# One kernel, eight layers: guest pieces in slots of their own, and in the state-space layer a fifth of the products on GpSimd and the convolution on TensorE

## The chip, the cores and the metric

The kernel runs on one core of one Trainium2 chip. The metric is the device time of one execution in microseconds (us), the median of three runs. Engines are named as the profile names them: PE is TensorE's matmuls and PEld its weight loads, DVE is VectorE, ACT is ScalarE, POOL is GpSimd, SP is SyncE, which here only issues transfers.

## The reference

A tensor `x` of 8 sequences of 256 tokens and 128 features goes through eight residual layers, `x = x + f(layernorm(x))`:

```
linear attention (16 heads, running sums)         -> feed-forward, 8 experts, top 2, plus a shared one
softmax attention (16 heads of 64)                -> the same feed-forward
causal attention with rotary positions (16 of 8)  -> feed-forward, 32 experts, top 4, at most 128 tokens each
state-space layer (below)                         -> the same feed-forward
```

The state-space layer, with 128 features `d` and 64 states `n`:

```
left, right = split(up_x @ W_up + b_up)
x     = silu(sum_k conv_w[:, k] * left shifted by k + conv_b)        # three taps in time
delta = softplus(x @ W_delta + b_delta)
Bm, Cm = x @ W_B + b_B, x @ W_C + b_C
h_t   = exp(delta_t * A[d, n]) * h_(t-1) + delta_t * Bm_t[n] * x_t[d]   # a scan over 256 tokens
y_t[d] = sum_n h_t[d, n] * Cm_t[n] + D_skip[d] * x_t[d]
out   = (y * silu(right)) @ W_down + b_down
```

## The kernel before

The tokens are cut into four passes of 512 (two sequences each). The eight layers run one after the other, each over its four passes; a layer's loop is its stage. In the order of the profile: linear attention (20 to 119 us), `biased_ffn` (119 to 308), `wide_attention` (308 to 666), `biased_ffn` again (666 to 857), `rotary_attention` (857 to 1081), `capped_ffn` (1081 to 1287), `state_space` (1287 to 1787) and `capped_ffn` again (1787 to 1986).

**Guests.** What has to be ready before a pass of a layer (layer norm, projections, routing) is cut into numbered pieces, `tensor(pe, p, n)`, `scalar`, `gpsimd` and `vector`, one function for each engine. While a stage works on pass p, its loop calls the pieces of its own pass p + 1, one piece number in each slot of the loop; in its last pass it calls the pieces of the next layer's first pass. `Following.slot(n)` does that, and the list `within` of the guest says how many pieces are done by each slot of its host. Every engine executes its queue in order, so a piece that has to wait holds up the host's work behind it on that engine. Between two stages all engines meet at the end of a block; SP's queue of transfers must have been issued by then.

**`capped_ffn`** has 17 slots in a pass. On PE iteration g does `up(g + 3)` (six matmuls), the guest piece, `spread_weights(g)` and `down(g - 2)`; on DVE it does `hidden(g + 3)`, `weigh(g)` and the guest piece. `route_vector` is the routing on DVE. Its part 4, in slot 11, applies the cap (four operations) and splits the weights into three bf16 parts (five operations); the PE piece of slot 13, `route_turn`, waits for the split (`r_split`) and transposes it.

**`biased_ffn`** has 9 slots. Its host loops on ACT change the table of functions for a guest's Ln and back: a layer norm's second half (`prepare_scalar(..., 1)`) waits for a PE matmul, loads a table, runs Ln and Exp, and the host loads its own table again.

**`rotary_attention`** as a guest: norm in pieces 6 to 8, four projections with their rotations in 9 to 12, in 12 also the key and its four masked copies `rot_km` on POOL, values in 13.

**`state_space`** has 64 slots, or steps, in a pass, each for two halves of the features and a fixed state group: a scan of [128, 512].

```
PE    spread_rows(i): exponent's delta -> bank DELTA[i % 3]; delta*x -> bank DELTA_X[i % 3]
ACT   exp of the first, in place
DVE   dbx(i) = bank DELTA_X * Bm (L2114); then the scan of step i - 1 (L2122)
POOL  hc(i) = h * Cm (L2078)
PE    reduce(i - 4): adds hc into bank 5 (L2024)
```

PE does `spread_rows(i)`, `reduce(i - HOLD)` and the guest piece, in this order. `spread_rows(i)` waits for the scan of i - 3, the scan of i for `hc` of i - 4. After a pass, DVE's `finish` needs all 64 reductions, and the next pass's first `reduce` waits for `gated`. The guest pieces on DVE: the convolution in three operations (17 to 19), silu in two (23, 24), the gate (25), softplus (31, 32, 36, 37), delta*x (38). `delta` and `delta*x` are split into three bf16 parts by ACT and POOL in turn (39 to 48), and then `sync` moves them into `packed` with twelve transfers on SP.

## Time and profile before

| what | value |
|---|---|
| time, median of 3 runs | 1993.4 us (1988.6 to 1994.98) |
| the profiled execution: its own time | 1988.01 us |
| its span, first to last instruction | 1986.2 us |
| PE busy | 1786.8 us, 90% |
| DVE busy | 1511.3 us, 76% |
| ACT busy | 874.8 us, 44% |
| POOL busy | 703.6 us, 35% |
| mean granted TensorE clock | 0.966 |

The busy shares are means over stages of different kinds. The granted clock has two levels, full (2.4 GHz, shown as 1.00) and half (1.2 GHz, shown as 0.50); a value between is a stretch with both. In a line of the timeline the number in brackets is how long the engine had been idle before, and what released it. A wait for several semaphores is put down to one of them.

### The profile page before, as it was taken

The numbers are of one execution on the slowest core, as the hardware profiler recorded it, in microseconds if no ns is written. First come the engines' busy times: TensorE is split into PE (matmuls) and PEld (weight loads), VectorE is DVE, ScalarE is ACT, GpSimd is POOL, SyncE is SP. The second block draws the span as 40 slices with busy tenths as digits, with TensorE's granted clock in tenths as the row PEclk, the third lists the DMA queues.
The fourth block names the chain that finished last, engine by engine and source line by source line (L and its number), as shares of the span: only waits on it lengthen the run. The fifth ranks groups of instructions, "written<-read, shape, count | busy, mean of one in ns | idle before, by whom it ended". The sixth has DMA issues, their size and how long they took to land. (4 is left out here: it accounts for less than half of the span.)

```text
span 1986.2 us, 23692 instructions
## 1 busy us (share of the span) xinstructions
PE 1786.8 (90%) x7574; PEld 932.4 (47%) x7581; DVE 1511.3 (76%) x2501; ACT 874.8 (44%) x2063; POOL 703.6 (35%) x802
## 2 busy tenths in 40 slices
PE   7879999999998999989998999888888888789999
PEld 2346654555554555546665555432222323225555
DVE  5868865555555588657767888699999999997887
ACT  3345544654545454345653333444354443333332
POOL 4722222333333222322220000077678686660000
PEclk9989999999999999979998999899999999999999
DMA  6000000000000000010000000000000000000000
GB/s 244 1 1 0 1 0 1 1 1 1 1 1 1 0 1 1 0 43 2 1 2 1 1 0 1 17 0 13 5 0 17 0 15 2 0 0 1 0 6 16
DMA packets 9787, 19.94 MB, mean 10 GB/s; under 512 B 1088, under 2 KB 8384, under 8 KB 8768
## 3 DMA queue, kind: packets, MB, share of 16 engines
q1 hardware_dynamic: 9664, 18.42, 2.7%
q8 instruction: 62, 1.02, 0.2%
q14 instruction: 61, 0.50, 0.1%
HBM read 14.22 MB, written 1.05 MB: 8 GB/s over the span
## 5 line engine op out<-in xcount | busy, mean ns | idle before, releaser
L2078 POOL TENSOR_TENSOR ssm_hc<-ssm_h,ssm_cm 128x512 f32<-128x512 f32 x256 | 334.6, 1309 | 155.2 <-DVE ssm_h L2122 154.9
L2122 DVE TENSOR_TENSOR_SCAN ssm_h<-banks,ssm_dbx 128x512 f32<-128x512 f32 x256 | 310.6, 1214 | 2.3 <-DVE ssm_dbx L2114 2.3
L307 PE MATMUL banks<-ffn_x_high,up_high 128*128 128x512 f32 x544 | 283.5, 521 | 13.9 <-ACT ffn_s1g L856 9.6
L2024 PE MATMUL banks<-ssm_hc,const 128*128 128x512 f32 x512 | 272.9, 615 | 12.2 <-DVE ssm_gated L2099 9.3
L2062 ACT ACTIVATE banks<-banks,a_neg 128x510 f32<-128x510 f32 x256 | 167.1, 659 | 248.0 <-PE banks L2011 247.1
L308 PE MATMUL banks<-ffn_x_low,up_high 128*128 128x512 f32 x544 | 216.9, 399 | 0.0
L309 PE MATMUL banks<-ffn_x_high,up_low 128*128 128x512 f32 x544 | 216.5, 398 | 0.0
L1498 POOL TENSOR_SCALAR wide_pin<-wide_pin,wide_rden 128x256 f32<-128x256 f32 x256 | 117.6, 478 | 226.1 <-DVE wide_rden L1516 226.1
L2114 DVE TENSOR_TENSOR ssm_dbx<-banks,ssm_bm 128x512 f32<-128x512 f32 x256 | 171.9, 672 | 13.5 <-PE banks L2014 11.4
L343 POOL TENSOR_TENSOR x_norm<-x_centred,x_square 128x512 f32<-128x512 f32 x32 | 41.3, 1291 | 395.1 <-ACT x_square L338 395.1
L1731 ACT ACTIVATE ffn_th<-banks 128x512 f32<-128x512 f32 (+1 forms) x136 | 81.1, 597 | 212.4 <-PE banks L309 190.2
L2011 PE MATMUL banks<-ssm_packed,half 96*128 96x510 bf16 x256 | 103.0, 402 | 75.8 <-DVE ssm_h L2122 71.1
L307 PEld LDWEIGHTS banks<-ffn_x_high,up_high 128*128 128x128 f32 x544 | 103.3, 190 | 103.1 <-issue 43.7
L1156 ACT ACTIVATE rot_pin<-banks,rot_low 128x128 f32<-128x128 f32 (+1 forms) x256 | 104.1, 419 | 99.9 <-DVE rot_low L1238 99.9
L2011 PEld LDWEIGHTS banks<-ssm_packed,half 96*128 96x128 bf16 x256 | 25.1, 98 | 256.8 <-DVE ssm_h L2122 231.2
L1696 PE MATMUL banks<-ffn_a,weights 128*128 128x512 f32 (+1 forms) x272 | 141.2, 602 | 0.0
L1767 DVE SCALAR_TENSOR_TENSOR ffn_p<-ffn_th,banks 128x512 f32<-128x512 f32 (+1 forms) x136 | 92.8, 683 | 59.2 <-ACT ffn_th L1731 58.4
L308 PEld LDWEIGHTS banks<-ffn_x_low,up_high 128*128 128x128 f32 x544 | 103.7, 191 | 50.9 <-issue 35.8
L2024 PEld LDWEIGHTS banks<-ssm_hc,const 128*128 128x128 f32 x512 | 100.0, 198 | 57.9 <-POOL ssm_hc L2078 20.3
L1472 ACT ACTIVATE wide_pin<-banks,wide_low 128x256 f32<-128x256 f32 x256 | 117.5, 478 | 13.4 <-DVE wide_low L1530 13.4
L882 POOL TENSOR_SCALAR ffn_hg<-ffn_hg 128x512 f32<-128x512 f32 x72 | 45.1, 627 | 203.4 <-DVE ffn_hg L904 202.1
L309 PEld LDWEIGHTS banks<-ffn_x_high,up_low 128*128 128x128 f32 x544 | 103.4, 190 | 25.4
(230 smaller groups left out, 3373.6 us busy)
## 6 DMA issues: line engine op xcount, KB each, us to landing
ssm_packed<-ssm_parts SPq DMA_DIRECT2D x48, 64.0 KB, 2.0
up_whole<-in_up SPq DMA_DIRECT2D x1, 2304.0 KB, 15.1
weights<-in_weights SPq DMA_DIRECT2D x1, 2048.0 KB, 22.4
up_whole<-in_up SPq DMA_DIRECT2D x1, 2048.0 KB, 8.5
half<-in_half SPq DMA_DIRECT2D x1, 1440.0 KB, 17.8
weights<-in_weights SPq DMA_DIRECT2D x1, 1168.0 KB, 24.7
weights<-in_weights SPq DMA_DIRECT2D x1, 1152.0 KB, 8.1
const<-in_const SPq DMA_DIRECT2D x1, 1042.0 KB, 10.0
```

The lines of the kernel that those rows point to most:

```text
L307: pe.matmul(out, w_high, x_high, start=True, stop=False)
L308: pe.matmul(out, w_high, x_low, start=False, stop=False)
L309: return pe.matmul(out, w_low, x_high, start=False, stop=True)
L1472: ins = act.activation(pin[:, i % RING, m, cols], k.bank[2 * (i % 2) + m][:, cols], ACT.Exp, bias=low[:, i % RING, n:n + 1], accum_out=den ...
L1498: ins = pool.tensor_scalar(part, part, rden[:, i % RING, n:n + 1], 1.0, ALU.mult, ALU.mult)
L1696: pe.matmul(k.bank[5][:], w("sd" if n == 0 else f"d{n - 1}")[0:rows, :], a[0:rows, g % (LAG + 1), :], start=(n == 0), stop=(n == N - 1)).t ...
L2011: pe.matmul(two(k.bank[DELTA[i % AHEAD]])[:, :, 1:], pick, two(packed[0:96, p % 2, 0, g, :])[:, :, 1:], start=True, stop=True) \
L2024: pe.matmul(k.bank[5][:], k.c("hot")[:, P - row:2 * P - row], hc[:, i % HOLD, :], start=(i % NP == 0), stop=(i % NP == NP - 1)).then_inc(s ...
L2062: act.activation(spot_i, spot_i, ACT.Exp, scale=k.a_neg[:, i % NP:i % NP + 1]).then_inc(s["da"], 1)
L2078: pool.tensor_tensor(hc[:, i % HOLD, :], h[:, i % HOLD, :], cm[:, i // NP % 2, :], ALU.mult) \
L2114: dve.tensor_tensor(dbx[:, i % AHEAD, :], k.bank[DELTA_X[i % AHEAD]][:], bm[:, i // NP % 2, :], ALU.mult) \
L2122: dve.tensor_tensor_scan(h[:, n % HOLD, :], k.bank[DELTA[n % AHEAD]][:], dbx[:, n % AHEAD, :], 0.0, ALU.mult, ALU.add).then_inc(s["h"], 1)
```

## The change

**Routing.** `route_vector` has seven parts instead of six: the split is a part of its own. In `capped_ffn` it moves from slot 11 to slot 12; `route_turn` stays in slot 13. In `biased_ffn` it stays in the same slot. The `within` lists of the guests are moved to fit, above all `biased_ffn` in `wide_attention`, whose pieces 3, 4, 5, 6 go to slots 10, 11, 12, 13 (before 8, 11, 13, 14 with 5 and 6 both in 14).

**Rotary guest.** ACT's half of the norm runs one slot behind PE's, all pieces behind it one later, and `rot_km` is made in two pairs in two more slots.

**State space.** Twelve of 64 products in a pass (steps 4, 9, ... 59) leave DVE: ACT copies the bank to `dxs`, POOL multiplies by Bm into `pdbx`, after `hc` of four steps earlier. PE's two spreads are issued apart, the one of delta*x a step earlier. The convolution is three fp32 matmuls with diagonal weights; ACT moves the result out with bias and the factor 0.5, so silu is one operation on DVE; `u = 1 + e` goes to ACT. The table for tanh is loaded in piece 19, the one for Ln in piece 34. The second and third split parts move from 43 to 48 to 47 to 54, and `sync` issues four transfers behind each part instead of twelve behind the last. `a_neg` is computed while the layer is a guest.

```
@@ route_vector
             link(dve.tensor_tensor(cw, cw, buf["rank"][:], ALU.mult))
+    if n == 5:
         link(dve.tensor_copy(part(0), buf["cw"][:]))
...
-    if n == 5:
+    if n == 6:
         dve.wait_ge(s["r_turned"], p + 1)
@@ biased_ffn, capped_ffn
-        for part in {4: (0,), 5: (1,), 6: (2, 3, 4), 7: (5,)}.get(n, ()):
+        for part in {4: (0,), 5: (1,), 6: (2, 3, 4, 5), 7: (6,)}.get(n, ()):
...
-"wide": (0,) * 7 + (1, 3, 3, 3, 4, 4, 5, 7, 8)},
+"wide": (0,) * 7 + (1, 3, 3, 4, 5, 6, 7, 7, 8)},
...
-        if n in (5, 6, 7, 8, 11, 13):
+        if n in (5, 6, 7, 8, 11, 12, 13):
@@ rotary_attention
-        if n == 7:
+        if n == 8:
             prepare_scalar(k, act, s, p, 1)
...
-            for c in range(4):
+        for c in {14: (0, 1), 15: (2, 3)}.get(n, ()):
...
-{"ffn0": (7, 8, 9, 10, 11, 12, 13, 14, 16)}
+{"ffn0": (7, 8, 10, 11, 12, 13, 14, 15, 16)}
@@ wide_attention
+                if follow.done >= 5:
+                    pe.wait_ge(nxt.s["r_diff"], 1)
@@ state_space, sync
-        sp.wait_ge(s["split"], 6 * (p + 1))
-        for g in range(4):
-            for part in range(3):
+        for part in range(3):
+            sp.wait_ge(s["split"], 6 * p + 2 * part + 2)
+            for g in range(4):
@@ state_space, guest pieces
+        if n == 19:
+            pe.wait_ge(s["right_in"], p + 1)
+            pe.wait_ge(s["cleared"], 1)
+            for tap in range(3):
+                ins = pe.matmul(two(k.bank[7]), w(f"conv{tap}"), left[:, :, tap:L + tap],
+                                start=(tap == 0), stop=(tap == 2))
+            ins.then_inc(s["conv"], 1)
...
+        if n == 20:
+            act.wait_ge(s["conv"], p + 1)
+            act.activation(conv[:], k.bank[7][:], ACT.Identity, bias=half_b[:], scale=0.5).then_inc(s["conv_in"], 1)
+        if n == 19:
+            k.table(act, "exp_and_others")
...
-            link(dve.scalar_tensor_tensor(conv[:], tc[:], 1.0, conv[:], ALU.add, ALU.mult))
-        if n == 24:
-            dve.tensor_scalar(xs[:, p % 2, :], conv[:], 0.5, None, ALU.mult).then_inc(s["x"], 1)
+            dve.scalar_tensor_tensor(xs[:, p % 2, :], tc[:], 1.0, conv[:], ALU.add, ALU.mult).then_inc(s["x"], 1)
@@ state_space, loop: PE, ACT, POOL, DVE
             for i in range(ALL + HOLD):
+                if i + 1 < ALL:
+                    spread_dx(i + 1)
                 if i < ALL:
-                    spread_rows(i)
+                    spread_delta(i)
...
+                if i + 1 < ALL and by_pool(i + 1):
+                    m = pooled[i + 1]
+                    act.wait_ge(s["bx"], i + 2)
...
+                    act.activation(dxs[:, m % 2, :], k.bank[DELTA_X[(i + 1) % AHEAD]][:], ACT.Copy).then_inc(s["dx_in"], 1)
...
+                j = i + AHEAD + 1
+                if j < ALL and by_pool(j):
+                    m = pooled[j]
+                    pool.wait_ge(s["dx_in"], m + 1)
...
+                    pool.tensor_tensor(pdbx[:, m % 2, :], dxs[:, m % 2, :], bm[:, j // NP % 2, :], ALU.mult) \
+                        .then_inc(s["pdbx"], 1)
...
-                if i < ALL:
-                    dve.wait_ge(s["bc"], 2 * i + 2)
+                if i < ALL and not by_pool(i):
+                    dve.wait_ge(s["bx"], i + 1)
```

## Rows read from the trace of the kernel before

**Rows 1.** Windows: us, busy time (instructions) by engine, clock, DMA; state-space stage.

```profile
1287.00:1787.00 500.00, 410.10 (x1102) 147.15 (x1102) 479.89 (x591) 211.42 (x329) 352.26 (x272) 0.96 0.02 6
```

**Rows 2.** Timeline of DVE: start, length, line; state-space stage, convolution and silu.

```profile
1319.57 1.21 DVE L2122 TENSOR_TENSOR_SCAN ssm_h<-banks,ssm_dbx 128x512 f32<-128x512 f32 x1
...
1321.86 1.22 DVE L2122 TENSOR_TENSOR_SCAN ssm_h<-banks,ssm_dbx 128x512 f32<-128x512 f32 x1
...
1326.73 1.22 DVE L2122 TENSOR_TENSOR_SCAN ssm_h<-banks,ssm_dbx 128x512 f32<-128x512 f32 x1
...
1328.44 1.22 DVE L2122 TENSOR_TENSOR_SCAN ssm_h<-banks,ssm_dbx 128x512 f32<-128x512 f32 x1
...
1332.16 1.21 DVE L2122 TENSOR_TENSOR_SCAN ssm_h<-banks,ssm_dbx 128x512 f32<-128x512 f32 x1
...
1334.60 1.21 DVE L2122 TENSOR_TENSOR_SCAN ssm_h<-banks,ssm_dbx 128x512 f32<-128x512 f32 x1
...
1336.64 1.21 DVE L2122 TENSOR_TENSOR_SCAN ssm_h<-banks,ssm_dbx 128x512 f32<-128x512 f32 x1
```

**Rows 3.** Chain that ended last, by time: start, length; second capped_ffn.

```profile
1834.35 0.42 PE banks L387 x4
...
1840.53 0.86 PE banks L1696 x2
...
1850.87 0.87 PE banks L322 x2
```

**Rows 4.** Timeline of POOL, state-space stage, end of its guest work in a pass.

```profile
1360.88 1.63 POOL L2078 TENSOR_TENSOR ssm_hc<-ssm_h,ssm_cm 128x512 f32<-128x512 f32 x1 [0.80 <-DVE ssm_h L2122]
...
1373.20 1.26 POOL L2078 TENSOR_TENSOR ssm_hc<-ssm_h,ssm_cm 128x512 f32<-128x512 f32 x1
1374.42 1.16 POOL L1941 TENSOR_TENSOR ssm_rest<-ssm_dx,ssm_parts 128x512 f32<-128x512 f32 x1
```

**Rows 5.** Waits of the state-space stage: total us, times, longest.

```profile
ACT ssm_parts L1931 <- POOL ssm_rest L1941: 23.5, 12, 3.1
```

**Rows 6.** Instructions with the tile ssm_gated: ns min/median/max.

```profile
L2099 DVE SCALAR_TENSOR_TENSOR ssm_gated<-ssm_y,ssm_gate x4: 692/1218/1220, 1415.2 to 1788.0; 128x512 f32<-128x512 f32 x4
```

**Rows 7.** Timeline between two passes of the state-space stage.

```profile
1415.21 1.22 DVE L2099 SCALAR_TENSOR_TENSOR ssm_gated<-ssm_y,ssm_gate 128x512 f32<-128x512 f32 x1
...
1416.58 1.75 PE L2024 MATMUL banks<-ssm_hc,const 128*128 128x512 f32 x2 [3.09 <-DVE ssm_gated L2099]
...
1420.70 0.69 DVE L2114 TENSOR_TENSOR ssm_dbx<-banks,ssm_bm 128x512 f32<-128x512 f32 x1 [2.54 <-PE banks L2014]
```

**Rows 8.** Timeline of SP, then ACT and PE, at the start of that stage.

```profile
1279.22 7.78 SPq L1848 DMA_DIRECT2D ssm_packed<-ssm_parts  x12
...
1287.74 0.26 ACT L2056 ACTIVATE a_neg<-weights 128x64 f32<-128x64 f32 x1 [7.24 <-PEq L1610]
...
1288.36 0.61 PE L2011 MATMUL banks<-ssm_packed,half 96*128 96x510 bf16 x1 [4.58 <-DVE banks L2093]
```

**Rows 9.** Timeline of capped_ffn, slots 11 to 13 of a pass.

```profile
1832.89 0.23 DVE L449 CAST r_split<-r_cw 128x128 bf16<-128x128 f32 x1
...
1834.21 0.68 DVE L1767 SCALAR_TENSOR_TENSOR ffn_p<-ffn_th,banks 128x512 f32<-128x512 f32 x1
...
1834.35 0.42 PE L387 MATMUL banks<-half,r_split 128*96 128x128 bf16 x4 [0.94 <-DVE r_split L453]
...
1836.12 0.68 DVE L1767 SCALAR_TENSOR_TENSOR ffn_p<-ffn_th,banks 128x512 f32<-128x512 f32 x1
```

**Rows 10.** Windows: stretches with and behind a wait of PE.

```profile
1256.50:1259.90 3.40, 3.40 (x6) 1.63 (x5) 1.81 (x3) 0.69 (x1) 0.00 (x0) 0.50 0.00 0
1832.00:1838.00 6.00, 5.06 (x20) 2.23 (x19) 5.66 (x15) 1.19 (x2) 0.00 (x0) 1.00 0.00 0
...
813.50:819.50 6.00, 6.00 (x14) 3.95 (x14) 4.57 (x7) 2.90 (x5) 1.84 (x3) 0.50 0.01 3
```

**Rows 11.** Timeline of PE in the first capped_ffn, last pass.

```profile
1255.80 1.46 PE L1873 MATMUL banks<-ssm_xs,weights 128*128 128x512 f32 x2 [2.34 <-DVE ssm_xs L1964]
```

**Rows 12.** Timeline of the second biased_ffn, guest norm and last pass's end.

```profile
813.47 0.79 PE L307 MATMUL banks<-ffn_x_high,up_high 128*128 128x512 f32 x1 [3.35 <-ACT ffn_s1g L856]
...
843.81 2.69 POOL L1016 TENSOR_SCALAR rot_km<-rot_k,const 128x512 f32<-128x512 f32 x4
...
850.38 3.84 PE L823 MATMUL banks<-ffn_a,weights 128*128 128x512 f32 x4 [5.12 <-DVE ffn_a L923]
```

**Rows 13.** Timeline of PE in wide_attention, last pass.

```profile
639.86 1.97 PE L1412 MATMUL banks<-wide_pt,wide_va 128*64 128x256 f32 x8 [4.75 <-DVE wide_pt L1525]
```

More of the change, by code:

```diff
@@ L1821, in state_space @@
     ALL = PASSES * NP
-    s = k.semaphores("ssm", ["left", "left_in", "right", "right_in", "tanh_r", "conv", "tanh_c", "x", "delta", "z", "e", "u",
+    by_pool = lambda i: i % NP % 5 == 4
+    pooled = [0]
+    for i in range(ALL):
+        pooled.append(pooled[-1] + by_pool(i))
+    steps = [i for i in range(ALL) if by_pool(i)]
+    s = k.semaphores("ssm", ["bx", "dx_in", "pdbx", "halved", "cleared", "conv_in", "left", "left_in", "right", "right_in", "tanh_r", "conv", "tanh_c", "x", "delta", "z", "e", "u",
                              "ln", "b", "b_in", "c", "c_in", "gate", "ready", "rest", "split", "packed0", "packed1", "packed2", "packed3",
@@ L1885, in scalar @@
             act.wait_ge(k.w_loaded[G], 16)
+            act.activation(k.a_neg[:], w("a_log"), ACT.Exp).then_inc(s["a"], 1)
         if n == 7:
@@ L1911, in scalar @@
             act.activation(e[:], e[:], ACT.Exp, scale=-1.0).then_inc(s["e"], 1)
+        if n == 30:
+            act.wait_ge(s["e"], p + 1)
+            act.activation(u[:], e[:], ACT.Identity, bias=1.0).then_inc(s["u"], 1)
         if n == 31:
@@ L1915, in scalar @@
         if n == 34:
+            k.table(act, "natural_log_exp_and_others")
             act.wait_ge(s["c"], p + 1)
@@ L1986, in run, with programs @@
         dbx = sb("ssm_dbx", [P, AHEAD, T])
+        dxs, pdbx = sb("ssm_dxs", [P, 2, T]), sb("ssm_pdbx", [P, 2, T])
         h, hc = sb("ssm_h", [P, HOLD, T]), sb("ssm_hc", [P, HOLD, T])
         with nc.Block(no_gpsimd_drain=True) as block:
[L1989 to L1991 removed]
+            programs(nxt, block, y, gated, dbx, dxs, pdbx, h, hc)
+    def programs(nxt, block, y, gated, dbx, dxs, pdbx, h, hc):
         @block.sync
@@ L2009, in spread_rows, with spread_dx @@
                     pe.wait_ge(s["h"], i - AHEAD + 1)
-                pick = k.h("pick")[0:96, c * P:(c + 1) * P]
-                pe.matmul(two(k.bank[DELTA[i % AHEAD]])[:, :, 1:], pick, two(packed[0:96, p % 2, 0, g, :])[:, :, 1:],
-                          start=True, stop=True) \
-                    .then_inc(s["bc"], 1)
-                pe.matmul(k.bank[DELTA_X[i % AHEAD]][:], pick, packed[0:96, p % 2, 1, g, :], start=True, stop=True) \
-                    .then_inc(s["bc"], 1)
+                pe.matmul(two(k.bank[DELTA[i % AHEAD]])[:, :, 1:], k.h("pick")[0:96, c * P:(c + 1) * P],
+                          two(packed[0:96, p % 2, 0, g, :])[:, :, 1:], start=True, stop=True).then_inc(s["bc"], 1)
+            def spread_dx(i):
+                (g, c), p = spot(i), i // NP
+                if c == 0:
+                    pe.wait_ge(s[f"packed{g}"], 16 * 3 * (p + 1))
+                if i >= AHEAD and by_pool(i - AHEAD):
+                    pe.wait_ge(s["dx_in"], pooled[i - AHEAD + 1])
+                elif i >= AHEAD:
+                    pe.wait_ge(s["dbx"], i - AHEAD + 1 - pooled[i - AHEAD + 1])
+                pe.matmul(k.bank[DELTA_X[i % AHEAD]][:], k.h("pick")[0:96, c * P:(c + 1) * P],
+                          packed[0:96, p % 2, 1, g, :], start=True, stop=True).then_inc(s["bx"], 1)
             def reduce(i):
@@ L2296 @@
     lay(5, "b_right", m["b_up"][P:, None])
-    lay(5, "conv_w", m["conv_w"])
+    for tap in range(3):
+        lay(5, f"conv{tap}", np.diag(m["conv_w"][:, tap]))
     lay(5, "conv_b", m["conv_b"][:, None])
```

103 lines of the change are left out of this document (51 added, 52 removed).

## The prediction, made before the changed kernel ran

> **What bounds the kernel now.** I read the busy time by stage first, then the timeline inside the stages that the change touches. The state-space stage is the longest, 500 us, and DVE is busy for 479.9 of them, PE for 410, POOL for 352 and ACT for 211 [rows 1]. In its timeline the scans follow each other: between two bare steps 1.71 us from start to start, of which the scan takes 1.13 and the product 0.58, and each guest operation of DVE pushes the next scan back by its own length [rows 2]. So time taken from DVE here is time taken from the kernel, until POOL or PE is next. The `capped_ffn` stages are different. The chain of waits runs there through PE from `route_turn` (L387) over `down` (L1696) to the next norm (L322), 16.5 us in which a matmul follows a matmul [rows 3]. What delays `route_turn` delays the kernel.
>
> **The products.** 48 of 256 leave DVE: 48 x 0.58 = 27.8 us less. What can take it back is POOL. Two of its operations in a row are 1.22 us apart for `hc`, 1.1 for the split's [rows 4]. A pass with guests then costs POOL 64 + 12 + 1 operations at 1.22 and 4 at 1.1, 98 us. DVE's pass is 64 x 1.13 + 52 x 0.58 = 102.5 and about 6 for its guests and `finish`. POOL has 0.7 us of slack in five steps (8.0 against 6 x 1.22 = 7.3). Steps 43 to 50 hold two pairs of split operations and two products: followed, the product of step 54 lands 0.7 us after its scan could start. I take 0.8 us in each of three passes, +2.5, bounds 0 and +20 (a rival below). ACT's 48 copies lie in its idle time.
>
> The Trainium skill (GPSIMD Engine Reference, Performance versus the Vector engine) keeps elementwise work on VectorE, GpSimd being 1.96 times slower. The rows here say 1.22 against 0.58, 2.1 times. By that rule the move is a bad trade, 58.6 us of POOL for 27.8 of DVE; by the rows of the stage POOL has 148 us idle and DVE 20, and I go with these.
>
> **DVE's guests.** Three taps of the convolution stretch three steps to 7.16 us where bare ones take 5.14: 2.02. Silu's two operations stretch two steps to 4.48 against 3.43, and the second alone costs 0.33 [rows 2]; the new silu keeps the first. `u` is of the second's kind, 0.33. That is 2.02 + 0.33 + 0.33 = 2.7 us in a pass, 8.0 in the three passes hosted here. The three matmuls are 3 x 0.87 = 2.6 us of PE in one slot [rows 3]; PE runs more than 2 us ahead of the scan, so I cost them at nothing here.
>
> **The shared path of DVE and POOL.** `gated`, which reads two SBUF tensors, takes 0.69 us once and 1.22 in three of four cases, with POOL at work [rows 6], and `hc` takes 1.63 instead of 1.26 beside such a guest of DVE [rows 4]. Today these guests start as a scan ends, when POOL is mostly idle; with POOL at 90% they will meet it halfway. Seven such operations in three passes, every second one late by 0.53: +5.6 us, bounds 0 and 11. The Trainium skill (SBUF — State Buffer, on the shared port pair) says that the pair is locked for a whole instruction and the loser blocks; the two lengths agree with it, and by it a meeting could cost up to a whole POOL operation.
>
> **Smaller waits of the stage.** ACT waits 23.5 us for POOL's split operations in 12 waits of up to 3.1 us [rows 5], some of which hold back the exponentials and through them a scan (0.4 us twice in a pass). Four to six slots between writer and reader remove these: -2. Between two passes the first `reduce` waits 3.09 us for `gated`, and DVE's product then 2.54 us for the spread queued behind it [rows 7]. With delta*x spread a step earlier, and step 68 a pooled one, DVE gets a step further before it stops: -1.1 at each of three borders, -3.3.
>
> **Start of the stage.** SP issues its twelve transfers in 7.78 us, until 1287.0, and the block can't end before; ACT starts at 1287.74 and PE, after `a_neg` and the resets, at 1288.36. PE had been idle since 1283.8 [rows 8]. With eight transfers issued behind the earlier parts, four remain, 2.6 us, done by 1281.8; the block ends with PE and DVE near 1283.9. -3.4 us.
>
> **The split behind part 4 of the routing.** Today DVE begins the split at 1832.89, goes on with `hidden(15)` at 1834.21, and PE, idle for 0.94 us, starts `route_turn` at 1834.35. The next `hidden` begins at 1836.12, so one `hidden` and one `weigh` take 1.91 us [rows 9]. The split now stands behind these two in DVE's queue, and PE still asks for it in slot 13, where its `up(16)` is already done. PE's wait grows from 0.94 to 2.85 us. All behind it is PE's own chain [rows 3], so the 1.91 us are paid: three passes in each of two stages, 6 x 1.91 = +11.5. Bursts on DVE get smaller, but DVE isn't what the 16.5 us behind wait for.
>
> Such a wait has a second price. PE waits 2.34 us at 1253.5 [rows 11], and the stretch 1256.5 to 1259.9 is granted 0.50 of the clock; after the 3.35 us at 810 it is 813.5 to 819.5; around today's 0.94 us the clock stays at 1.00 [rows 10]. A 2.85 us wait is between the two longer ones. With 3.4 us at half speed PE does 1.7 us less: 6 x 1.7 = +10.2, bounds 0 and +20.
>
> **Rotary guest in the second `biased_ffn`.** PE waits 3.35 us for `s1`, because ACT sits in the norm's second half (its wait, two table loads, Ln, Exp) [rows 12]. A slot later the matmul is long done, ACT's 3.9 us fall where PE works on `up(31)`, and wait and half clock go: 3.35 + 3.4 = -6.7, bounds -3 and -7. At the stage's end PE waits 5.12 us; the clamp that it needs stood behind `rot_km`, 2.69 us on POOL [rows 12]. Two at a time, behind two clamps: -2.5, bounds -1 and -4.
>
> **Routing guest in `wide_attention`.** Slot 14 holds all of the routing, 4.2 us of DVE without a pause, and PE waits 4.75 us [rows 13], then runs at half clock. In slots 12 and 13 I expect 1.6 and 0.9 us instead: 2.2 less, and some of the clock back. -4, bounds -2 and -7.
>
> **State-space guest in the first `capped_ffn`.** The convolution adds 2.6 us to PE where PE is the bound. Against that, one round of two table loads goes, which was behind the 2.34 us [rows 11]: of it I leave 0.9, and with it goes the half clock, 1.7. Loading Ln's table before a wait saves about 0.5. Sum -1.0, bounds -4 and +2.6.
>
> **The sum.** -27.8 + 2.5 - 8.0 + 5.6 - 2.0 - 3.3 - 3.4 + 11.5 + 10.2 - 6.7 - 2.5 - 4.0 - 1.0 = -28.9 us, on the profiled execution's 1988.0: 1959.1. The median of the runs is 5.4 us above that execution. From the median it would be 1964.5; I predict 1963, between the two and nearer the median.
>
> **Rivals.**
>
> *The turn costs little.* The clock may hold through a wait of 2.85 us (the windows at 0.50 begin behind the wait, and two cases are few), and DVE's other meetings with POOL may be free. Then -28.9 - 10.2 - 5.6 = -45: 1948. For it: no spell after 0.94 us. Against: two of two longer waits have one. 0.2.
>
> *POOL becomes the bound of the state-space stage.* POOL waits in order for a copy that comes over PE and ACT, and PE waits for POOL's `hc` in the `reduce` ahead of that spread. Once POOL lags, this circle (reduce 0.87, a guest matmul 0.87, spread 0.2, copy 0.66, hand-overs 0.3: 2.9 us) is longer than the 2.44 us of two POOL operations that cover it. If that gives back half of the 27.8 us and a little more, the result is -12: 1980. For it: slack of only 0.7 us in five steps. Against: without guests the lag never builds up. 0.2.
>
> *Slower.* The same circle, if it never recovers: a POOL wait of w in every period of five steps makes the period 7.3 + w, and with w above 1.3 us it is as long as today's 8.57. All 27.8 us are then gone, and from w = 1.4 on the kernel is slower; at w = 2, 51 x 0.7 = 36 us are added and the result is about 2029. The circle above gives w of at most 0.5 from rows. 0.06, other causes included.
>
> *The change does nothing that can be measured*, as where the losses in `capped_ffn` (up to 32 us) meet a half-lost gain: within 6 us (0.3%, about what this kernel's measurement can tell) of 1993. 0.05.
>
> **How the numbers follow.** The forecast (1951 to 1974) has 0.49, the two milder rivals 0.2 and 0.2. Both are faster by over 0.3%: 0.89. The range 1944 to 1982 leaves out about 2 in 10: the slower case, no change, and the outer parts of the two rivals.
>
> **What the profile after would show.** Right: bare scans 1.13 us apart twelve times in a pass; the state-space stage near 467 us with DVE above 90% and POOL near 85%; PE idle between the stages under 1.5 us; at L387 in `capped_ffn` a wait of 2.8 us six times, with 0.50 of the clock soon after, and each such stage 10 us longer; no wait of 3.35 us before `up(31)` in the second `biased_ffn`. Wrong: DVE waiting for POOL's product or for `da` at most pooled steps (then POOL is the bound), a turn that waits 1 us, or guests of DVE that keep their lengths.

## The result, and the profile after

| kernel | median | ratio to before, 95% interval | profiled span |
|---|---|---|---|
| before, timed beside it | 1989.5 us (1988.5 to 1995.0, 5 runs) | | 1986.2 us |
| changed | 1978.7 us (1976.2 to 1981.6, 5 runs) | 0.9944 (0.9927 to 0.9961) | 1976.9 us |

The change makes the kernel 0.56% faster, 10.9 us, where 30 us were predicted. First the page of the changed kernel, its line of busy time:

```profile
PE 1798.7 (91%) x7598; PEld 946.4 (48%) x7605; DVE 1485.6 (75%) x2434; ACT 901.3 (46%) x2117; POOL 755.8 (38%) x850
```

Where the time went, stage by stage. Each stage ends with the first of two matmuls that follow its last residual; their start times, before and after, cut the two traces at the same places:

| stage | before | after | difference | forecast |
|---|---|---|---|---|
| linear attention and first `biased_ffn` | 307.4 | 309.7 | +2.3 | 0 |
| `wide_attention` | 354.3 | 349.1 | -5.2 | -4.0 |
| second `biased_ffn` | 193.7 | 187.9 | -5.8 | -9.2 |
| `rotary_attention` | 224.1 | 225.0 | +0.9 | 0 |
| first `capped_ffn` | 203.7 | 210.6 | +6.9 | +9.8 |
| `state_space` | 507.7 | 487.6 | -20.1 | -36.4 |
| second `capped_ffn` | 190.9 | 202.6 | +11.7 | +10.8 |

Most of what is missing, 16 us of 20, is missing in the state-space stage. The windows of the changed kernel (columns as in [rows 1]), first that stage, then stretches of PE at half clock:

```profile
1282.50:1770.10 487.60, 416.14 (x1126) 160.28 (x1125) 456.80 (x531) 239.48 (x382) 402.88 (x320) 0.95 0.02 6
...
1166.50:1173.30 6.80, 6.47 (x12) 2.03 (x13) 3.18 (x7) 0.59 (x1) 0.00 (x0) 0.51 0.00 0
1221.20:1224.60 3.40, 3.40 (x6) 0.75 (x4) 1.07 (x3) 0.56 (x1) 0.00 (x0) 0.54 0.00 0
1815.10:1818.50 3.40, 3.40 (x9) 1.29 (x8) 1.95 (x4) 0.00 (x0) 0.00 (x0) 0.54 0.00 0
1866.30:1873.10 6.80, 6.43 (x12) 2.02 (x13) 3.23 (x7) 0.59 (x1) 0.00 (x0) 0.52 0.01 2
1920.90:1924.30 3.40, 3.40 (x6) 0.85 (x5) 1.60 (x3) 0.00 (x0) 0.00 (x0) 0.53 0.00 0
838.90:862.80 23.90, 20.27 (x84) 10.20 (x83) 9.26 (x16) 8.78 (x34) 6.63 (x7) 0.51 0.25 89
```

DVE is busy 94% of the state-space stage and POOL 83%, much as forecast; the stage is 487.6 us all the same. So the loss isn't to be seen in busy shares.

**The turn.** The timeline of DVE, then of PE, where [rows 9] had 0.94 us:

```profile
1813.39 0.22 DVE L450 CAST r_split<-r_cw 128x128 bf16<-128x128 f32 x1
...
1814.56 0.23 DVE L454 CAST r_split<-r_rest 128x128 bf16<-128x128 f32 x1
```

```profile
1814.84 0.66 PE L387 MATMUL banks<-half,r_split 128*96 128x128 bf16 x4 [2.85 <-DVE r_split L454]
```

The wait is there six times, 2.83 to 2.85 us, and behind five of the six stands one of the half-clock windows above (the first, at 1113.8, has none). The forecast for the wait was 2.85 us.

**The state-space stage**, timeline of SP, PE and DVE at its start:

```profile
1281.53 1.24 SPq L1859 DMA_DIRECT2D ssm_packed<-ssm_parts  x2
...
1283.75 0.61 PE L2039 MATMUL banks<-ssm_packed,half 96*128 96x512 bf16 x2 [0.87 <-DVE banks L2132]
...
1285.45 1.22 DVE L2165 TENSOR_TENSOR_SCAN ssm_h<-banks,ssm_dbx 128x512 f32<-128x512 f32 x1
```

The first scan starts 3.2 us behind the end of the stage before; in the kernel before it was 7.7: -4.5 (forecast -3.4); SP is no longer behind the others, as it was in [rows 8]. At the borders between two passes, timelines of PE and DVE:

```profile
1406.49 2.05 PE L2049 MATMUL banks<-ssm_hc,const 128*128 128x512 f32 x2 [3.55 <-DVE ssm_gated L2138]
```

```profile
1404.88 1.46 DVE L2138 SCALAR_TENSOR_TENSOR ssm_gated<-ssm_y,ssm_gate 128x512 f32<-128x512 f32 x1
...
1410.71 0.69 DVE L2153 TENSOR_TENSOR ssm_dbx<-banks,ssm_bm 128x512 f32<-128x512 f32 x1 [1.52 <-PE banks L2039]
```

PE's wait is longer than the 3.09 us of [rows 7], in part by the longer `gated` (1.46 us instead of 1.22); DVE's is 1.52 instead of 2.54, as the spread a step earlier was to bring. The loss comes behind all this. One place in the first pass shows how, in the timelines of POOL, PE and DVE, steps 14 to 21:

```profile
1309.53 1.27 POOL L343 TENSOR_TENSOR x_norm<-x_centred,x_square 128x512 f32<-128x512 f32 x1
1310.75 3.72 POOL L2110 TENSOR_TENSOR ssm_hc<-ssm_h,ssm_cm 128x512 f32<-128x512 f32 x3
1316.35 1.27 POOL L2123 TENSOR_TENSOR ssm_pdbx<-ssm_dxs,ssm_bm 128x512 f32<-128x512 f32 x1 [1.88 <-ACT ssm_dxs L2091]
```

```profile
1310.85 1.12 PE L1877 MATMUL banks<-x_norm,weights 128*128 128x512 f32 x2 [1.32 <-POOL x_norm L343]
...
1317.85 2.74 PE L1885 MATMUL banks<-ssm_left,weights 128*128 128x512 f32 x6
```

```profile
1312.23 0.69 DVE L2153 TENSOR_TENSOR ssm_dbx<-banks,ssm_bm 128x512 f32<-128x512 f32 x1 [1.11 <-PE banks L2039]
...
1316.91 1.22 DVE L2165 TENSOR_TENSOR_SCAN ssm_h<-banks,ssm_dbx 128x512 f32<-128x512 f32 x1 [0.79 <-issue]
...
1320.84 0.69 DVE L2153 TENSOR_TENSOR ssm_dbx<-banks,ssm_bm 128x512 f32<-128x512 f32 x1 [0.99 <-PE banks L2039]
```

A late POOL gives `x_norm` late, PE waits for it with the spreads queued behind, and DVE waits for the spread; a few steps on the six instructions of the convolution, 2.74 us on PE, do the same. And DVE's guests with two SBUF inputs are longer (groups: ns min/median/max; first `fix` in the kernel before, then the changed kernel):

```profile
L1974 DVE SCALAR_TENSOR_TENSOR ssm_fix<-ssm_u,ssm_e x4: 669/672/684, 1266.3 to 1597.7; 128x512 f32<-128x512 f32 x4
```

```profile
L1986 DVE SCALAR_TENSOR_TENSOR ssm_gate<-ssm_gate,ssm_right x4: 684/1352/1356, 1258.7 to 1570.2; 128x512 f32<-128x512 f32 x4
...
L1990 DVE SCALAR_TENSOR_TENSOR ssm_fix<-ssm_u,ssm_e x4: 684/1568/1583, 1267.7 to 1582.9; 128x512 f32<-128x512 f32 x4
...
L1995 DVE SCALAR_TENSOR_TENSOR ssm_delta<-ssm_z,ssm_fix x4: 691/1126/1128, 1272.9 to 1593.2; 128x512 f32<-128x512 f32 x4
...
L2138 DVE SCALAR_TENSOR_TENSOR ssm_gated<-ssm_y,ssm_gate x4: 691/1461/1466, 1404.9 to 1767.9; 128x512 f32<-128x512 f32 x4
```

The 684 ns are from `capped_ffn`, where POOL is idle. `ssm_gated` was 1218 in [rows 6]; `gate`, `fix` and `delta` took 0.67 us in this stage of the kernel before; they take 1.35, 1.57 and 1.13 now. A timeline of POOL and DVE shows one such meeting:

```profile
1342.43 1.27 POOL L2123 TENSOR_TENSOR ssm_pdbx<-ssm_dxs,ssm_bm 128x512 f32<-128x512 f32 x1
1342.67 1.58 DVE L1990 SCALAR_TENSOR_TENSOR ssm_fix<-ssm_u,ssm_e 128x512 f32<-128x512 f32 x1
```

`fix` begins inside POOL's operation, which ends at 1343.70, and ends 0.55 us behind it. All 15 guests of the first three passes that begin inside an operation of POOL do so, five in a pass; in the kernel before it was the three `gated` alone.

**A measure for the stage.** From the start of the first scan to that of the last there are 255 intervals. Bare, they would take 255 x 1.71 = 436.05 us, less 0.58 for each pooled product. What a kernel needs beyond that I call its excess. Two pairs of runs below have the same code in this stage (69.6 and 71.3, 40.7 and 38.6), so differences of 2 us in it say nothing. It comes from this group of DVE, before and after (read the two times behind the durations):

```profile
L2122 DVE TENSOR_TENSOR_SCAN ssm_h<-banks,ssm_dbx x256: 1194/1214/1225, 1290.9 to 1783.4; 128x512 f32<-128x512 f32 x128
```

```profile
L2165 DVE TENSOR_TENSOR_SCAN ssm_h<-banks,ssm_dbx x208: 1191/1212/1225, 1285.4 to 1763.3; 128x512 f32<-128x512 f32 x104
```

492.5 - 436.05 = 56.4 us before, 477.9 - (436.05 - 27.8) = 69.6 us after. The measure takes the forecast's 27.8 us for the bare pattern as given; in the trace 30 of the 48 intervals without a product on DVE are near 1.13 us, and the other 18 are in the excess. The excess grew by 13.2, where the forecast's terms (guests -8.0, split -2.0, borders -3.3, POOL late +2.5, meetings +5.6) had it shrink by 5.2.

### The profile page after: what moved, and what is told of

The parts are those of the page before. It is cut to its first block and busy times, and to the rows that moved or that the text cites. A ratio compares the mean times of both kernels' runs of the same rounds, so it can differ in the third digit from the quotient of the medians.

```text
span 1976.9 us, 23849 instructions
## 1 busy us (share of the span) xinstructions
PE 1798.7 (91%) x7598; PEld 946.4 (48%) x7605; DVE 1485.6 (75%) x2434; ACT 901.3 (46%) x2117; POOL 755.8 (38%) x850
## 5 line engine op out<-in xcount | busy, mean ns | idle before, releaser
L2110 POOL TENSOR_TENSOR ssm_hc<-ssm_h,ssm_cm 128x512 f32<-128x512 f32 x256 | 327.3, 1296 | 58.0 <-DVE ssm_h L2165 57.0
L2049 PE MATMUL banks<-ssm_hc,const 128*128 128x512 f32 x512 | 281.2, 631 | 33.9 <-POOL ssm_hc L2110 23.1
L307 PE MATMUL banks<-ffn_x_high,up_high 128*128 128x512 f32 x544 | 282.6, 519 | 10.3 <-ACT ffn_s1g L857 6.2
L2165 DVE TENSOR_TENSOR_SCAN ssm_h<-banks,ssm_dbx 128x512 f32<-128x512 f32 x208 | 249.4, 1211 | 10.6 <-ACT banks L2094 5.5
L2153 DVE TENSOR_TENSOR ssm_dbx<-banks,ssm_bm 128x512 f32<-128x512 f32 x208 | 138.9, 668 | 11.6 <-PE banks L2039 10.8
L2049 PEld LDWEIGHTS banks<-ssm_hc,const 128*128 128x128 f32 x512 | 98.6, 200 | 79.0 <-POOL ssm_hc L2110 56.4
L2039 PE MATMUL banks<-ssm_packed,half 96*128 96x512 bf16 x256 | 100.8, 394 | 7.8 <-DVE ssm_dbx L2153 6.5
```

What stands on the lines that cost most here:

```text
L307: pe.matmul(out, w_high, x_high, start=True, stop=False)
L2049: pe.matmul(k.bank[5][:], k.c("hot")[:, P - row:2 * P - row], hc[:, i % HOLD, :], start=(i % NP == 0), stop=(i % NP == NP - 1)).then_inc(s ...
L2110: pool.tensor_tensor(hc[:, i % HOLD, :], h[:, i % HOLD, :], cm[:, i // NP % 2, :], ALU.mult) \
L2153: dve.tensor_tensor(dbx[:, i % AHEAD, :], k.bank[DELTA_X[i % AHEAD]][:], bm[:, i // NP % 2, :], ALU.mult) \
L2165: dve.tensor_tensor_scan(h[:, n % HOLD, :], k.bank[DELTA[n % AHEAD]][:], product, 0.0, ALU.mult, ALU.add).then_inc(s["h"], 1)
```

## The experiments

Each run has the kernel before timed beside it; the ratios are what is compared. The scans and the excess come from one profiled execution, which is within 2.5 us of the median except with the convolution on DVE (8.5 us under it) and the early spread (3.8 under).

| run | median us | ratio, 95% | scans, us | excess |
|---|---|---|---|---|
| changed kernel | 1978.7 | 0.9944 (0.9927 to 0.9961) | 477.9 | 69.6 |
| split in slot 11 | 1960.1 | 0.9854 (0.9842 to 0.9867) | 479.6 | 71.3 |
| no pooled products | 1977.6 | 0.9938 (0.9926 to 0.9951) | 476.8 | 40.7 |
| convolution on DVE | 1979.7 | 0.9949 (0.9933 to 0.9966) | 476.0 | 67.8 |
| convolution in three slots | 1978.4 | 0.9947 (0.9935 to 0.9959) | 479.3 | 71.1 |
| exponential first | 1985.0 | 0.9984 (0.9975 to 0.9993) | 483.4 | 75.2 |
| early spread | 1978.2 | 0.9952 (0.9936 to 0.9969) | 474.1 | 65.9 |
| idle operations on POOL | 1990.3 | 1.0003 (0.9991 to 1.0016) | 489.4 | 53.4 |
| quiet places, split in 11 | 1944.5 | 0.9781 (0.9766 to 0.9795) | 462.6 | 47.9 |
| quiet places in all passes | 1940.1 | 0.9756 (0.9738 to 0.9775) | 460.2 | 43.8 |
| busy places | 1961.0 | 0.9862 (0.9844 to 0.9880) | 481.2 | 66.6 |
| quiet, convolution on DVE | 1941.0 | 0.9766 (0.9747 to 0.9785) | 462.5 | 44.4 |
| split in 11, no products | 1954.0 | 0.9828 (0.9809 to 0.9847) | 474.6 | 38.6 |

**The split in slot 11.**

```
-        if n in (5, 6, 7, 8, 11, 12, 13):
+        for part in {5: (0,), 6: (1,), 7: (2,), 8: (3,), 11: (4, 5), 13: (6,)}.get(n, ()):
```

> The changed kernel with one thing undone: in capped_ffn the split (part 5 of the routing on DVE) stands in slot 11 again, behind part 4, and no longer in slot 12 behind hidden and weigh. Theory 'the turn waits behind one hidden and one weigh, and pays for it twice': PE's wait ahead of route_turn falls from 2.85 us to about 0.94 in all six passes, 6 x 1.91 = 11.5 us less, and the stretches of half clock behind it (five of the six have one, 3.4 or 6.8 us long, 23.9 us together) go as well, 12 us less. Together 23 us less than the changed kernel: near 1956 us, ratio to the kernel before 0.983. Rival 'only the wait counts': the half-clock stretches have other causes and stay, 11.5 us less, near 1967, ratio 0.9886. Rival 'the turn isn't on the path': less than 3 us.

The ratio falls by 0.0090, 18 us. The first `capped_ffn` goes from 210.6 to 200.2 us and the second from 202.6 to 191.2: 21.8 us, of which 6 x 1.91 = 11.5 are the wait; the remaining 10.3 go with the half-clock windows, which are gone. The state-space stage gave 2.5 back. The waits of the second `capped_ffn` for the split (total us, times, longest), changed kernel and this one:

```profile
PE banks L387 <- DVE r_split L454: 8.5, 3, 2.9
```

```profile
PE banks L387 <- DVE r_split L454: 2.8, 3, 0.9
```

Inside either `capped_ffn` no stretch is at half clock now, but for the first 2 us of the second. Both prices of the turn hold.

**No pooled products.**

```
-    by_pool = lambda i: i % NP % 5 == 4
+    by_pool = lambda i: False
```

> The changed kernel without the twelve pooled products in a pass: all 256 products on DVE, no copies to dxs, everything else as changed. By the terms of the forecast (48 products 27.8 us, of which the shared path took 5.6 and a late POOL 2.5 back) it is 19.7 us slower than the changed kernel: 1998 us, ratio 1.004. By the reading of the changed kernel's trace, in which the guests of DVE are longer by some 9 us in sum, the steps of the norm by 2 and the steps of the split by 4.3, it is only about 12 us slower: 1990 us, ratio 1.000. If POOL is truly the bound of the stage the products are worth nothing and it is within 3 us of the changed kernel. In the trace the lengths of the fix, gate and delta operations on DVE should fall from 1.57, 1.35 and 1.13 us back to 0.67 if POOL's products are what they meet; the burst of six convolution matmuls should still push the scans back (by 2.3 us in a pass), if PE's short lead is the cause.

The time is that of the changed kernel. 27.8 us more of work on DVE, 28.9 us less excess. Of the cases in the expectation it is the last: the products are worth nothing. The groups of the guests:

```profile
L1986 DVE SCALAR_TENSOR_TENSOR ssm_gate<-ssm_gate,ssm_right x4: 662/663/683, 1260.9 to 1569.3; 128x512 f32<-128x512 f32 x4
...
L1990 DVE SCALAR_TENSOR_TENSOR ssm_fix<-ssm_u,ssm_e x4: 661/662/684, 1269.8 to 1581.8; 128x512 f32<-128x512 f32 x4
```

They are back at 0.66 us, so POOL's products are what made them long. The convolution costs 1.09 us a pass, not the 2.3 that I expected: half of its loss was POOL's too. The excess by place, us, worked out from the starts of the 256 scans (guest pieces of the first three passes; the last pass apart):

| steps, with their guests | before | changed | no products | quiet, all passes |
|---|---|---|---|---|
| 0 to 6, border | 17.1 | 13.3 | 11.9 | 10.0 |
| 7 to 13, norm | 0.0 | 2.5 | 0.3 | 0.0 |
| 14, 15, projection behind x_norm | 2.7 | 4.7 | 0.0 | 0.2 |
| 16 to 20, convolution | 6.1 | 7.1 | 3.3 | 6.4 |
| 21 to 25, silu, gate | 5.3 | 6.2 | 3.6 | 3.6 |
| 26 to 38, softplus | 9.1 | 12.0 | 8.0 | 8.0 |
| 39 to 63, split | 3.2 | 7.9 | 0.2 | 1.6 |
| last pass, from step 7 | 12.8 | 15.9 | 13.3 | 13.9 |

The third column against the first is the change without its headline: 15.7 us less excess. The second against the third is what 48 products cost: something at every guest.

**The convolution, back on DVE, or in three slots of PE.**

```
-        if n == 19:
+        if n in (19, 20, 21):
...
-            for tap in range(3):
...
+            pe.matmul(two(k.bank[7]), w(f"conv{tap}"), left[:, :, tap:L + tap],
+                      start=(tap == 0), stop=(tap == 2)).then_inc(s["conv"], 1)
...
```

These are the three slots of PE. The version on DVE has the three taps in its pieces 17 to 19 again.

> The changed kernel with the convolution on DVE again, three taps in pieces 17 to 19 (with halved weights, so that silu stays one operation), and no conv matmuls and no copy on ACT. Theory 'PE has no lead to spare': the three matmuls hold up the spreads behind them, and the scans around them lose 0.87 + 1.46 = 2.33 us in each of the three passes; taps on DVE cost 2.04. So the state-space stage changes by less than 1.5 us in sum, and the first capped_ffn, where PE is the bound, is 2.6 us shorter: 2 to 4 us less than the changed kernel, 1975 us. The forecast's pricing (matmuls free, taps 2.02 each pass) says 6.1 - 2.6 = 3.5 us more: 1982 us.

> The changed kernel with the three convolution matmuls in three slots (pieces 19, 20, 21) instead of all in 19, and ACT's copy, its tanh and silu one or two pieces later. Theory 'PE has no lead to spare': a slot then needs 1.30 + 0.87 = 2.17 us of PE against 1.71 of DVE, so PE falls back by 0.46 in each of three slots instead of 2.2 at once; the scans of these steps lose about 0.9 us in a pass instead of 2.33: 3 to 4 us less than the changed kernel in three passes, 1975 us. The forecast's view (the matmuls were free anyway) says no difference, within 1 us. A rival within the theory: as DVE runs at PE's pace there, it could save nothing, if each of the three slots takes 2.17 us.

On DVE: no difference in time that can be told (0.9949 against 0.9944). The trace has the 2.9 us less in the first `capped_ffn` (207.7), but the taps don't cost 2.04 us a pass. The group:

```profile
L1976 DVE SCALAR_TENSOR_TENSOR ssm_conv<-ssm_left,ssm_half_w,ssm_conv x4: 753/1534/1539, 1246.9 to 1553.0; 128x512 f32<-128x512 f32 x4
```

1.53 us instead of 0.73, since with a product on POOL in every fifth step the taps meet it too; they cost 3.84 us a pass, 4.4 us more in three passes than the matmuls. The steps of the split lose 3.0 us instead of 7.9 in that trace, so the sum hardly moves; why was not looked into. In three slots: no gain; the steps behind lost what the burst had lost (excess 71.1). That was the rival within the theory. Neither place is better while POOL is late.

**The order of copy and exponential, and the circle.**

```
+                act.wait_ge(s["bc"], i + 1)
...
+                act.activation(spot_i, spot_i, ACT.Exp, ...).then_inc(s["da"], 1)
                 if i + 1 < ALL and by_pool(i + 1):
...
```

> The changed kernel with ACT's exponential of step i ahead of the copy to dxs for step i + 1, instead of behind it. A copy holds an exponential back by 0.5 to 0.6 us. Theory 'the exponentials behind a copy are late' (interval 17 of each pass, 0.87 us, and interval 7, up to 1.09): most of 2.6 + 2.0 us comes back, 3 us less than the changed kernel. Theory 'POOL's time is what runs out': the copy comes 0.6 us later to a POOL that is late anyway, so what the exponentials gain POOL loses: within 1.5 us of the changed kernel.

```
-                if i + 1 < ALL:
+                if i + 1 < ALL and not by_pool(i + 1):
                     spread_dx(i + 1)
                 if i < ALL:
                     spread_delta(i)
+                if i + 2 < ALL and by_pool(i + 2):
+                    spread_dx(i + 2)
...
```

> The changed kernel with PE's spread of delta*x for a pooled step issued one slot earlier, ahead of a reduce and a guest matmul instead of behind them, and ACT's copy right behind the exponential two steps ahead. This cuts the circle hc, reduce, guest, spread, copy, product. Theory 'the circle is what costs': POOL's 26.2 us of waiting for dxs fall below 8, PE waits less for hc, and the state-space stage is 8 to 12 us shorter (1968 us). Theory 'POOL's occupied time is what costs' (a product makes POOL late for the next steps, and whatever guest falls there pays): the waits for dxs go, but the scans hardly move, 0 to 3 us less.

How long POOL's product waited for the copy (us, times), in the changed kernel, with the exponential first, and with the early spread:

```profile
POOL ssm_pdbx L2123 <- ACT ssm_dxs L2091: 26.0, 17, 3.2
```

```profile
POOL ssm_pdbx L2123 <- ACT ssm_dxs L2094: 55.0, 39, 3.7
```

```profile
  ACT ssm_dxs L2096: 9.4, 13
```

A copy 0.6 us later is worse by 5.6 us of excess, and outside both cases that I gave (0.9984, and 6 us more in the median): POOL's lateness matters more than an exponential's. The early spread takes two thirds of the waits away and shortens the scans by 3.8 us in its trace, in the medians nothing (0.9952 against 0.9944). So the circle over reduce, guest, spread and copy is at most some 4 of the 29 us. What of the rest is POOL's occupied time alone?

**Idle operations on POOL.**

```
-    by_pool = lambda i: i % NP % 5 == 4
+    by_pool = lambda i: False
...
+                if i % NP % 5 == 0 and i % NP < 60:
+                    pool.tensor_tensor(pdbx[:, i // 5 % 2, :], bm[:, i // NP % 2, :], cm[:, i // NP % 2, :], ALU.mult)
```

> The kernel without pooled products (all 256 on DVE), but with twelve operations of the same size a pass on POOL (Bm * Cm into pdbx, which nobody reads), at the places where the products stood. They wait for nothing and nobody waits for them, so this measures what POOL's time alone costs, without the copy on ACT and the way over PE. In the kernel without products the stage's scans had 40.7 us above the bare pattern, with products 69.6. Theory 'POOL's occupied time costs': most of the 28.9 us is here too, 15 to 25 us more than without products, 1993 to 2003 us. Theory 'the circle over PE and ACT costs': only the meetings of DVE's two-input guests with POOL are paid, 7 us, and something for x_norm behind an operation: 6 to 10 us, 1984 to 1988 us. Since DVE has more work here (no product less), POOL has 0.6 us more in five steps, which speaks for the lower end of either.

1990.3 us: 12.7 more than without them, 12.7 in the excess as well (53.4 against 40.7). That lies between the two expectations. 3.9 of it is in the softplus steps, where `fix` and `delta` meet POOL again, 3.1 in the split's, 2.9 in the last pass. So 48 operations that nobody waits for cost DVE 0.26 us each. The other 16.2 us of the products' 28.9 come with their being needed: scans wait for them, ACT has a copy each, and DVE, 0.58 us faster in five steps, leaves POOL less time to catch up. Which of the three has how much wasn't taken apart.

**Places for the products.** If a product costs by what falls behind it, it is a matter of where it stands. POOL runs the product of step j behind `hc(j - 4)` and is late for some steps from there. Free of guests are only eight places in a pass:

```
...
-    by_pool = lambda i: i % NP % 5 == 4
+    QUIET = ((4, 9, 20, 30, 43, 49, 55, 59, 63), (12, 20, 30, 43, 49, 55, 59, 63), (12, 20, 30, 43, 49, 55, 59, 63),
+             (4, 9, 14, 19, 24, 29, 34, 39, 44, 49, 54, 59))
+    by_pool = lambda i: i % NP in QUIET[i // NP]
```

> The split of capped_ffn in slot 11, and pooled products only where no guest falls into the four steps before: steps 12, 20, 30, 43, 49, 55, 59, 63 of the second and third pass, these with 4 and 9 for 12 and 20 of the first, every fifth as before in the last (where the guests are capped_ffn's). 37 products instead of 48. Theory 'a product costs by what falls into the steps behind it': 37 x 0.58 = 21.5 us are taken from DVE and about a third goes back, so 12 to 16 us less than with every fifth (1960): 1944 to 1948 us, ratio 0.978. If the products cost what they give wherever they stand, it is 1960 again, and if the last pass or the borders are where the losses lie, 1955.

1944.5 us, 0.9781: as expected. Then the last pass in the same manner (9, 14, 19, 37, 41, 49, 54, 59, 63), and against it the control with products just ahead of guests:

> The version with quiet places (1944.5 us) with two changes: in the first pass step 12 instead of 9, and in the last pass steps 9, 14, 19, 37, 41, 49, 54, 59, 63, away from the border and from capped_ffn's pieces on DVE (34 products in all). Theory 'a product costs by what falls into the steps behind it': the first pass loses 0.5 us of its excess, the last 4 of its 21.5 us, against 3 x 0.58 = 1.7 us of products given up: 2.5 to 3 us less, 1942 us, ratio 0.9765. If the places in the last pass are without influence, 1.7 us more: 1946 us.

> The version with quiet places again with the same number of products (37), but in the first three passes at places where a guest falls right behind each: steps 8, 15, 21, 27, 34, 39, 47, 53 (and 4 in the first pass) instead of 12, 20, 30, 43, 49, 55, 59, 63. Theory 'a product costs by what falls into the steps behind it': its 8 products a pass give back about what they take, as with every fifth (0.6 to 0.7 us each), so it is 25 x 0.6 = 12 to 16 us slower than the quiet version: 1957 to 1960 us, ratio 0.985. Theory 'only the number counts' (48 are too many for POOL, 37 are not): the same as the quiet version within 2 us, 1944 us.

> The quiet version with the better last pass and with the convolution on DVE again, and no product at step 20, whose wake would fall on the taps (31 products). The taps should now be as short as in the kernel before, 2.04 us in a pass instead of the 1.7 to 1.8 that the burst of six matmuls costs in the quiet version; in the first capped_ffn PE has 2.6 us less: 3 x 0.3 + 3 x 0.58 - 2.6 = 0, so the same as the quiet version with the better last pass, within 1.5 us. If the taps meet POOL anyhow (3.84 us a pass, as with every fifth product), 5 us slower than it.

> The changed kernel with the split of capped_ffn in slot 11 and no pooled products at all. It is the base against which the quiet version (34 products, ratio 0.9756) and the version with busy places (37 products, ratio 0.9862) are to be read. If the two edits are independent, it is 18 us less than without products (ratio 0.9938 - 0.0090 = 0.985, 1959 us). Then the 34 products at quiet places are worth 19 of their 19.7 us, and 37 at busy places nothing. If it comes out near 0.976 instead, the quiet version owes its gain to something else.

The groups of scans in the version quiet in all passes, and in the one with busy places (from the first start of the one line to the last of the two):

```profile
L2167 DVE TENSOR_TENSOR_SCAN ssm_h<-banks,ssm_dbx x222: 1193/1209/1225, 1276.4 to 1735.5; 128x512 f32<-128x512 f32 x111
L2167 DVE TENSOR_TENSOR_SCAN ssm_h<-banks,ssm_pdbx x34: 1194/1209/1225, 1282.7 to 1736.6; 128x512 f32<-128x512 f32 x34
```

```profile
L2167 DVE TENSOR_TENSOR_SCAN ssm_h<-banks,ssm_dbx x219: 1189/1208/1225, 1276.8 to 1758.0; 128x512 f32<-128x512 f32 x110
```

460.2 and 481.2 us. The medians are 1940.1 us (1942 expected) and 1961.0 (1957 to 1960). Against the same kernel without products (38.6 of excess, 0.9828), 34 quiet products give 19.7 us and cost 5.3: 14.4 net, and the ratios say 0.0072, 14.3 us. 37 at busy places give 21.5 and cost 28.1: a loss of 6.6, and the ratios say 0.0034, 6.8 us. The nearest pair has 37 products each and the same last pass: quiet places 1944.5 us with 47.9 of excess, busy places 1961.0 with 66.6. It is the place, not the number. My base was 5 us too high, and with it the worth that I expected of the quiet ones (19 us).

The traces do say how the excess divides into longer operations of DVE and idle time of DVE. Windows from the first scan to the last (columns as in [rows 1]), in this order: changed kernel, no products, idle operations; and, with the split in slot 11, no products, quiet in all passes, busy places:

```profile
1285.45:1763.27 477.82, 409.52 (x1109) 158.50 (x1109) 452.10 (x522) 238.71 (x381) 400.40 (x318) 0.95 0.02 6
1287.62:1764.38 476.76, 406.43 (x1109) 150.48 (x1109) 469.21 (x570) 215.56 (x333) 345.84 (x270) 0.97 0.02 6
1287.57:1777.04 489.47, 412.78 (x1109) 154.82 (x1109) 478.58 (x570) 215.78 (x333) 402.11 (x318) 0.95 0.02 5
...
1278.00:1752.61 474.61, 406.20 (x1109) 151.15 (x1109) 468.07 (x570) 215.55 (x333) 345.77 (x270) 0.97 0.02 6
1276.40:1736.57 460.17, 398.02 (x1108) 154.09 (x1107) 448.91 (x536) 231.40 (x367) 382.70 (x304) 0.97 0.02 6
1276.80:1758.02 481.22, 407.23 (x1109) 157.39 (x1109) 460.74 (x533) 234.90 (x370) 388.33 (x307) 0.95 0.02 5
```

| against the same kernel without products | DVE busy longer | DVE idle longer |
|---|---|---|
| products in every fifth step | 452.1 + 27.8 - 469.2 = 10.7 | 25.7 - 7.6 = 18.2 |
| idle operations | 9.4 | 3.3 |
| 34 quiet products | 448.9 + 19.7 - 468.1 = 0.6 | 11.3 - 6.5 = 4.7 |
| 37 products, busy places | 460.7 + 21.5 - 468.1 = 14.1 | 20.5 - 6.5 = 13.9 |

So POOL's time alone costs mostly by meetings, and what needed products add to it is nearly all waiting of DVE.

The convolution on DVE makes no difference here (0.9766). The taps are as short as before, since POOL is idle beside them:

```profile
L1978 DVE SCALAR_TENSOR_TENSOR ssm_conv<-ssm_left,ssm_half_w,ssm_conv x4: 725/727/750, 1237.2 to 1535.0; 128x512 f32<-128x512 f32 x4
```

The version that is quiet in all passes, 1940.1 us, beats both kernels: 2.4% under before, 1.9% under the changed one.

## Why the prediction was off

**Right.** The start of the stage (-4.5, forecast -3.4), the borders (17.1 to 13.3 us, -3.8, forecast -3.3), the turn (11.5 of wait and about 10 of clock, forecast 11.5 and 10.2), and, in the kernel without products, the split's steps (-3.0, forecast -2.0) and the small guests of DVE (silu and softplus -2.8, forecast -2.0). The routing guest in `wide_attention` has the right sign, and PE's wait is 2.04 us there instead of the 4.75 of [rows 13]; its size isn't settled. The stage is 5.2 us shorter here (forecast -4), but the 13 traces with this code have 349.1 to 353.4 us, in the median 352.2, 2.1 us under the one trace of the kernel before.

**The step that failed** is the paragraph "The products" with "The shared path". It gave back 2.5 us for a late POOL and 5.6 for meetings, 8.1 together. Measured, by leaving the products out: 28.9, all that they bring. Of these 10.7 are longer operations of DVE, against the 5.6 for meetings, and 18.2 are idle time of DVE, against the 2.5 for a late POOL. I weighed POOL against DVE by sums, over a pass and over five steps, found 0.7 us of slack, and followed only steps 43 to 50. What I found there came out in two of the three passes, where the scan of step 54 waits 0.71 and 0.74 us for its product. The other places were left out. POOL follows DVE step by step, and after an extra 1.22 us it is late for two or three steps, as it gains 1.71 - 1.22 = 0.49 us in each. Whatever stands in these steps pays: a guest on DVE that meets it (0.2 to 0.9 us longer), a projection behind `x_norm`, a burst on PE, the split. With products in every fifth step and guests in every second or third, nearly each product has such a neighbour.

Within that, the meetings were counted as every second of seven in a pass at 0.53 us. The trace has five of the seven in every pass, longer than before by 0.2 (`xs`, `gated`) to 0.9 us (`fix`), 7.4 us in three passes; the other two keep their length. The last pass brings 1.5 us more; what is left of the 10.7 is small and spread out. The Trainium skill (SBUF — State Buffer, on the shared port pair) says that a DVE operation with two SBUF inputs and a GpSimd one that reads SBUF exclude each other for a whole instruction; the trace agrees, 0.67 us where `fix` begins ahead of POOL's operation against 1.57 where it begins inside one, and 0.55 us from the end of the one to the end of the other. By the rule of the Trainium skill that elementwise work belongs on VectorE (GPSIMD Engine Reference, Performance versus the Vector engine) the products were a bad trade. As the change places them, they are an even one; at quiet places, a good one.

**The second step that failed**: "PE runs more than 2 us ahead of the scan, so I cost them at nothing here". A spread waits for the scan or the product of three steps ago, so PE can't be further ahead than that, and its own 1.30 us in a step of 1.71 (two spreads of 0.22 and a reduce of 0.87 from start to start) leave it 0.41 us a step to catch up. The burst costs 1.09 us a pass even with an idle POOL (3.3 us in three), more with products. That this short lead is the cause fits the burst, the three slots and the version on DVE, none of which gains; no run gave PE a longer lead. With the taps' 6.1 us gone the convolution gives 2.8 us with an idle POOL, not 6.1; as it was changed, it gives nothing (7.1 us against 6.1).

**The rival** "POOL becomes the bound" named the total (1980) and the stage, and said for it the circle. The circle is at most some 4 us, so that its total came out is luck. What it left out is that POOL's time alone costs DVE 12.7 us, and that waits come behind guests too. The sign that the prediction gave for this rival, DVE waiting at most pooled steps, did not show either: scans wait 26 times in the changed kernel, 12 of them at one of the 48 pooled steps or the step ahead of one, and twice for a product.

**Terms off in size.** The second `biased_ffn` gained 5.8 us instead of 9.2. The 3.35 us wait is gone, but at the end of the stage PE still waits twice, and the half clock behind it stays (838.9 to 862.8 above). Timelines of PE and of POOL:

```profile
838.42 1.91 PE L824 MATMUL banks<-ffn_a,weights 128*128 128x512 f32 x2 [2.41 <-DVE ffn_a L924]
842.23 2.07 PE L824 MATMUL banks<-ffn_a,weights 128*128 128x512 f32 x2 [1.90 <-DVE ffn_a L924]
```

```profile
835.95 2.25 POOL L1018 TENSOR_SCALAR rot_km<-rot_k,const 128x512 f32<-128x512 f32 x2
```

Two copies take 1.12 us each, where four took 0.67 each in [rows 12], and the 5.12 us have become 2.41 + 1.90: the saving of 2.5 was 0.8. These copies met DVE: in the trace its `ffn_p` and `ffn_a` run beside the four of this place, and the other twelve, with 0.69 us each, are as long as all sixteen before. In the first `capped_ffn` the state-space guest gave 3.5 us (200.2 us with the split in slot 11, against 203.7) instead of 1.0. The first two stages are 2.3 us longer; with the changed kernel's code there they took 307 to 310 us in these runs, so I give that no cause. `rotary_attention` likewise took 223.1 to 227.0 us. In the first `capped_ffn` the 2.34 us wait of [rows 11] is gone.

Left open: of the 16.2 us that needed products cost beyond idle ones, 1.3 are longer operations of DVE and 14.9 its idle time; how these are shared among waiting for products, ACT's copies and POOL's shorter slack isn't known.

## What to carry to other kernels

An engine that serves the critical one step by step has no slack to be added up over a pass: price each operation that you give it by what stands in the two or three steps behind it, and place it where nothing does. The same 0.58 us moved was worth 0.4 us at a quiet place and -0.2 at a busy one. Run the change without its main part before you believe in the main part: here all of the gain in this stage came from the small edits, and one small edit elsewhere, a split one slot later, had taken 18 us of it away.
